# One more probability chunk turned by DMA in a graph-attention kernel, with its buffers, score sums and row statistics rearranged

## The reference

```python
# layer 0
anchor_adj = jnp.einsum('md,de,ne->mn', x, weight, input)       # 6144 x 6144
scores = jnp.where(adj > 0, anchor_adj, NEG_PAD)
l0 = softmax(scores / 0.07, axis=1) @ input
x = layernorm(x + l0)
# layer 1
Wh = x @ W;  s1 = Wh @ a1;  s2 = Wh @ a2
e = leaky_relu(s1[:, None] + s2[None, :], 0.2)
h = softmax(where(adj > 0, e, -9e15), axis=1) @ Wh
x = layernorm(x + elu(h))
```

## Time and profile before

| | |
|---|---|
| profiled execution | 1458.37 us |
| its span | 1456.6 us |
| PE busy | 1411.4 us, 97% |
| VectorE busy | 1253.8 us, 86% |
| ScalarE busy | 1066.9 us, 73% |
| GpSimd busy | 1217.3 us, 84% |
| granted TensorE clock, mean of the span | 0.989 |
| DMA, mean | 200 GB/s; in stage 1 about 265 GB/s |

### The profile page before, as it was taken

The page is one execution under the profiler, slowest core; times in us unless marked ns, Lnnn a source line. Parts: engine busy times, 40 slices in busy tenths (PEclk is TensorE's granted clock), DMA queues, the critical chain, the costliest instruction groups (busy, mean ns, idle before and its releaser), DMA issues.

```text
span 1456.6 us, 28346 instructions
## 1 busy us (share of the span) xinstructions
PE 1411.4 (97%) x9661; PEld 1010.5 (69%) x9661; DVE 1253.8 (86%) x2129; ACT 1066.9 (73%) x2435; POOL 1217.3 (84%) x906
## 2 busy tenths in 40 slices
PE   8799999999999999999999999979999999999995
PEld 4577777777777777777777777755666666666664
DVE  6799999999999899999999999849898897979794
ACT  6688888888888888888888888868755555545453
POOL 6978888888888888888888888838999999999995
PEclk9999999999999999999999999988999999999998
DMA  8799999999999999999999998673434343434420
GB/s 267 243 286 261 271 253 266 273 266 275 273 256 264 249 272 267 270 271 271 266 256 265 261 261 268 185 140 66 107 68 103 85 102 85 104 67 111 76 58 14
DMA packets 427918, 291.38 MB, mean 200 GB/s; under 512 B 356864, under 2 KB 403200, under 8 KB 427776
## 3 DMA queue, kind: packets, MB, share of 16 engines
q1 hardware_dynamic: 427776, 289.59, 73.0%
HBM read 160.56 MB, written 40.89 MB: 138 GB/s over the span
## 4 chain that ended last, share of the span: by engine, by line
PE 92%; DVE 2%; POOL 2%; issue 1%; ACT 1%; DMA 1%; SPq 0%; POOLq 0%; ACTq 0%; DVEq 0%
PE ps L594 16%; PE ps L680 13%; PE ps L673 12%; PE ps L620 11%; PE ps L596 8%; PE ps L633 8%; PE ps L632 8%; PE ps L631 8%; PE ps L657 6%; PE ps L691 1%; POOL edges L426 1%; PE ps L564 1%; DVE rows L934 1%; POOL inp_sb L416 1%; POOL vals L419 0%
## 5 line engine op out<-in xcount | busy, mean ns | idle before, releaser
L798 ACT ACTIVATE rows<-rows,exp_bias 128x512 f32<-128x512 f32 x576 | 417.2, 724 | 58.2 <-DVE exp_bias L987 58.2
L505 POOL TENSOR_TENSOR p_lo<-p,p_hi 128x1024 fp32r<-128x1024 f32 x180 | 423.7, 2395 | 21.8 <-ACT p_hi L832 11.5
L934 DVE CUSTOM_DVE_ANT_0 rows<-ps,neg_mask 128x1024 f32<-128x1024 f32 x288 | 352.2, 1223 | 81.9 <-PE ps L633 71.1
L1014 DVE SCALAR_TENSOR_TENSOR p<-ps,e_col,edgesT 128x1024 f32<-128x1024 f32 x288 | 349.6, 1276 | 53.4 <-PE ps L650 36.5
L426 POOL TENSOR_SCALAR edges<-neg_mask 128x1536 uint8<-128x1536 bf16 x192 | 311.2, 1621 | 92.7 <-DVE neg_mask L909 80.7
L832 ACT CAST p_hi<-p 128x1024 fp32r<-128x1024 f32 x180 | 185.1, 1047 | 166.5 <-DVE p L1014 163.9
L594 PE MATMUL ps<-vals,pT_hi 128*128 128x256 f16 x1536 | 295.9, 273 | 3.1 <-DVE pT_lo L943 2.1
L784 ACT CAST pT_hi<-ps 128x512 f16<-128x512 f32 x384 | 222.7, 580 | 93.2 <-PE ps L620 93.0
L457 POOL TENSOR_TENSOR inp_sb<-rows,inp_sb 128x512 f16<-128x512 f32 x192 | 279.5, 1475 | 10.5 <-ACT inp_sb L792 2.9
L596 PE MATMUL ps<-vals,pT_lo 128*128 128x128 f16 x1536 | 275.1, 219 | 0.0
L943 DVE TENSOR_TENSOR pT_lo<-ps,pT_hi 128x512 f16<-128x512 f32 x384 | 250.8, 683 | 11.7 <-ACT pT_hi L784 11.7
(11 more groups left out here) (110 smaller groups left out, 1853.1 us busy)
## 6 DMA issues: line engine op xcount, KB each, us to landing
adj_sb<-adj SPq DMA_DIRECT2D x192, 768.0 KB, 5.7
edge_rows<-edges SPq DMA_DIRECT2D x192, 192.0 KB, 4.8
xq<-x SPq DMA_DIRECT2D x48, 64.0 KB, 2.9
xr<-x SPq DMA_DIRECT2D x48, 64.0 KB, 5.8
out<-y_w SPq DMA_DIRECT2D x5, 512.0 KB, 3.6
inp_sb<-inp SPq DMA_DIRECT2D x3, 768.0 KB, 8.2
inp_sb<-inp_sb SPq DMA_TRANSPOSE x96, 4.7
edgesT<-edge_rows SPq DMA_TRANSPOSE x48, 5.3
```

The source lines that it names most:

```text
L505: nc.gpsimd.tensor_tensor(p1_lo[:, m % LO_SLOTS, :], p1[:, (NB * g + n) % P_SLOTS, :], p1_hi[:, m % HI_SLOTS, :].bitcast(F32), ALU.subtrac ...
L798: nc.scalar.activation(row_chunk(1 - par, c), row_chunk(1 - par, c), ACT.Exp, bias=exp_bias[:, 1 - par:2 - par], scale=EXP_SCALE, accum_ou ...
L934: nc.vector.tensor_tensor_reduce(row_pair(par, k), scores_pair(k), neg_mask_row[:, 2 * k * CHUNK:2 * (k + 1) * CHUNK], 1.0, -3.0e38, ALU.a ...
L1014: nc.vector.scalar_tensor_tensor(out=p1[:, (NB * g + n) % P_SLOTS, :], in0=ps[:, R_ROW:R_ROW + 2, :].rearrange("p b w -> p (b w)"), scalar ...
```

## The change

- `MOVED` goes from 4 to 5: five of twelve chunks are split in SBUF and turned by DMA, seven by TensorE.
- `movedT` has one set instead of two. It is filled in two parts, chunks 0 to 2 and chunks 3 and 4, each with its own semaphore, so SP issues four DMA transposes a tile instead of two. Each part waits until TensorE has used the same chunks of the tile before.
- GpSimd makes a fifth low half, between the edges of quarters 0 and 1 of the next tile.
- GpSimd no longer multiplies `x1` by the weight rows and ScalarE no longer sums the products. VectorE does both in two instructions a tile, at step 7 (`SUMS_STEP`).
- `x1_total` is gone. TensorE sums all `x1` rows itself, one product of width 1 a tile, 46 of them in call t = 48.
- VectorE takes the row statistics of a tile at step 0 of the next call. GpSimd's power and `x1` move to the start of its next call. For the last tile VectorE does the two additions and `x1`.

```diff
-MOVED = 4
+MOVED = 5
+MOVED_PARTS = ((0, 3), (3, 5))
-        movedT = inp_space[:, 2 * MW:6 * MW].rearrange("p (s h b m) -> p s h b m", s=2, h=2, m=P)
+        movedT = inp_space[:, 2 * MW:4 * MW].rearrange("p (h b m) -> p h b m", h=2, m=P)
@@ SyncE
-                    after(sp, pv_done, C * (tile - 1))
-                    sp.dma_start_transpose(movedT[:, par, 0], moved_hi).then_inc(movedT_in[par], 16)
-                    sp.wait_ge(moved_lo_set, MOVED * (tile + 1))
-                    sp.dma_start_transpose(movedT[:, par, 1], moved_lo).then_inc(movedT_in[par], 16)
+                    for k, (a, b) in enumerate(MOVED_PARTS):
+                        after(sp, pv_done, C * (tile - 1) + (C - MOVED) + b if tile >= 1 else 0)
+                        for half, of, ready in ((0, moved_hi, moved_hi_set), (1, moved_lo, moved_lo_set)):
+                            sp.wait_ge(ready, MOVED * tile + b)
+                            sp.dma_start_transpose(movedT[:, half, a * BPC:b * BPC, :], of[:, a * CHUNK:b * CHUNK]
+                                                   ).then_inc(movedT_in[k], 16)
@@ GpSimd
+            def rstd_of_tile(tile):
+                pool.wait_ge(ve_set, tile + 1)
+                nc.gpsimd.tensor_tensor(small[:, 4:5], small[:, 3:4], consts[:, 0:1], ALU.pow).then_inc(rstd_set, 1)
             def tile_rstd(t, par, known):
+                if t >= 3:
+                    tile = t - 3
+                    rstd_of_tile(tile)
+                    pool.wait_ge(rstd_set, tile + 1)
+                    nc.gpsimd.tensor_scalar(x1_all[:, tile, :], xr[:, 1 - par, :], moments[:, 0:1], small[:, 4:5], ALU.subtract,
+                                            ALU.mult).then_inc(x1_set, 1)
...
+                if moved:
+                    moved_low(t - 1, 4)
+                if ahead:
                     make_edges(t + 1, 1)
...
-                    pool.wait_ge(ve_set, tile + 1)
...
-                    score_cols(tile)
@@ TensorE
+            def mean_part(j):
+                pe.wait_ge(x1_set, j + 1)
+                return nc.tensor.matmul(mean_ps, x1_all[:, j, :], averager[:, 0:1], start=(j == 0), stop=(j == NB - 1),
+                                        skip_group_check=True)
             def tile_steps(t, par, known):
                 for c in range(C):
+                    if t == NB:
+                        for j in range(4 * c, min(4 * c + 4, NB - 2)):
+                            mean_part(j)
@@ VectorE
+            def row_statistics(tile):
+                dve.wait_ge(u_set, tile + 1)
...
+            def score_sums(j):
+                dve.wait_ge(x1_set, j + 1)
+                dve.wait_ge(wa_copied, 1)
+                after(dve, s_set, 2 * j)
+                for k in range(2):
+                    nc.vector.tensor_tensor_reduce(s_prod[:, k, :], x1_all[:, j, :], wa_rep[:, k, :], 1.0, 0.0, ALU.mult,
+                                                   ALU.add, s_cols[:, k, j:j + 1]).then_inc(s_set, 1)
             def tile_steps(t, par, known):
                 for c in range(C):
+                    if c == 0 and t >= 3:
+                        row_statistics(t - 3)
...
+                    if c == SUMS_STEP and t >= 3:
+                        score_sums(t - 3)
```

More of the change, by code:

```diff
@@ L156, in build @@
         SPARE = EX0
-        VALS_BANKS = (2, 3, OUT3)
+        VALS_BANKS = (2, 3, SPARE)
+        mean_ps = ps[:, OUT3, 3 * P:3 * P + 1]
         def vals1_ps(k):
@@ L225, in build @@
         moved_hi_set, moved_lo_set = sem("moved_hi_set"), sem("moved_lo_set")
-        movedT_in = [sem(f"movedT_in{i}") for i in range(2)]
+        movedT_in = [sem(f"movedT_in{i}") for i in range(len(MOVED_PARTS))]
         att_out = sem("att_out")
@@ L285, in movedT_loads, with moved_part @@
         def movedT_loads(tile):
-            return 32 * (tile // 2 + 1)
+            return 32 * (tile + 1)
+        def moved_part(i):
+            return next(k for k, (a, b) in enumerate(MOVED_PARTS) if a <= i < b)
         def tiles(eng, body):
@@ L490, in tile_rstd @@
                     nc.gpsimd.tensor_tensor(xr[:, par, :], att[:, P:2 * P], xr[:, par, :], ALU.add).then_inc(u_set, 1)
-                    pool.wait_ge(ve_set, tile + 1)
[L492 to L495, removed]
-                    score_cols(tile)
             tiles(pool, tile_rstd)
+            rstd_of_tile(NB - 1)
             def low_part(g, n):
@@ L753, in _ @@
             z_high(1)
-            def score_sums(j):
-                act.wait_ge(s_prod_set, j + 1)
-                for k in range(2):
-                    op = nc.scalar.activation(s_prod[:, k, :], s_prod[:, k, :], ACT.Copy, accum_out=s_cols[:, k, j:j + 1])
-                op.then_inc(s_set, 1)
             def tile_steps(t, par, known):
@@ L901, in xT_low @@
                                                in1=xT_hi[:, par, :], op0=ALU.mult, op1=ALU.subtract).then_inc(xT_lo_set, 1)
+            def row_statistics(tile):
+                dve.wait_ge(u_set, tile + 1)
+                after(dve, x1_set, tile)
+                nc.vector.bn_stats(stats[:], xr[:, tile % 2, :]).then_inc(stats_set, 1)
+                dve.wait_ge(stats_set, tile + 1)
+                nc.vector.bn_aggr(moments[:], stats[:]).then_inc(moments_set, 1)
+                dve.wait_ge(moments_set, tile + 1)
+                nc.vector.tensor_scalar(small[:, 3:4], moments[:, 1:2], EPS, None, ALU.add).then_inc(ve_set, 1)
+            def score_sums(j):
[5 more added lines that the diff above has]
+                                                   ALU.add, s_cols[:, k, j:j + 1]).then_inc(s_set, 1)
             def make_mask(t, q, known):
@@ L970, in tile_steps @@
                                                     ALU.mult).then_inc(scaled_set, 1)
[L971 to L979 removed]
+                        if c == ATT_STEP + 1 and t == NB + 1:
+                            dve.wait_ge(att_out, NB)
+                            dve.wait_ge(xr_in[par], 16 * (t // 2))
+                            nc.vector.tensor_tensor(xr[:, par, :], att[:, 0:P], xr[:, par, :], ALU.add).then_inc(u1_set, 1)
+                            dve.wait_ge(u1_set, NB)
+                            nc.vector.tensor_tensor(xr[:, par, :], att[:, P:2 * P], xr[:, par, :], ALU.add).then_inc(u_set, 1)
                     if c == C - 1 and scores_of(known):
@@ L990, in _ @@
             tiles(dve, tile_steps)
-            dve.wait_ge(s_set, NB)
+            row_statistics(NB - 1)
+            dve.wait_ge(rstd_set, NB)
+            nc.vector.tensor_scalar(x1_all[:, NB - 1, :], xr[:, (NB - 1) % 2, :], moments[:, 0:1], small[:, 4:5], ALU.subtract,
+                                    ALU.mult).then_inc(x1_set, 1)
+            score_sums(NB - 1)
+            dve.wait_ge(s_set, 2 * NB)
             nc.vector.reduce_max(s_top[:, 0:1], s_cols[:, 0, :], AX_X).then_inc(s_part, 1)
```

59 lines of the change are left out of this document (17 added, 42 removed).

## The result

The changed kernel took 1487.42 us (median of 4 runs, 1486.24 to 1488.53), the kernel before 1458.35 us beside it (4 runs, 1456.67 to 1458.68): ratio 1.0201, interval 1.0187 to 1.0215. That is 29 us slower, where 1502 (1460 to 1528) had been forecast. The profiled execution has a span of 1486.6 us, 30.0 more than before.

The account below looks back on a forecast made before the run. A VectorE-GpSimd loop, nearly equal to TensorE's 19.35 us tile, would set the pace: 18.93 - 0.25 + 1.20 + 0.38 = 20.26. 1458.4 + 41 (45 tiles) + 3 (end of stage 1) = 1502 us, range 1460 to 1528.

Parts of the forecast that it names:

- the loop GpSimd, VectorE, GpSimd: Stage 1: edges to additions, statistics to mask, edges again; 18.93 us alone, 20.26 a tile after the change.
- The signs that were named for it: Middle tile: edges 20.2 us apart, VectorE idle over 1 us before statistics, TensorE gap at step 2, GpSimd chain 15.1 to 15.5.
- Statistics not opened by the move, row maximum ahead: VectorE's statistics still wait for GpSimd's additions; row maximum and bias go ahead of them, -0.25 us a tile.
- the slack: Free time in the loop of the kernel before: 0.42 us a tile of 19.35.
- The fifth low half: GpSimd, between mask and additions: adds its bare 1.20 us to the loop; could be 1.5 with stretching.
- The score sums: VectorE's two sums at step 7 hold up GpSimd's low halves: 0.38 us a tile, ends 0 and 0.56.
- The rate taken from the masks: VectorE masks stretch GpSimd by 0.68 us per us of mask; applied to 0.56 us of score sums.
- End of stage 1: Calls 48 and 49 and the chain to stage 2: +4.5, +0.7 and -2, together +3 us, between 0 and +5.
- TensorE as the limit: Rival: the loop has unseen slack, TensorE still sets stage 1's tile at 18.91 us; 1442 us; chance 0.13.
- VectorE held up by the sums: Rival: score sums wait for GpSimd instructions, VectorE sets the tile at about 20.8 us; 1526 us; chance 0.18.
- VectorE's busy time: In the rival with VectorE as limit: 17.6 + 2.7 = 20.3 us a tile, with waits about 20.8.
- The DMA: Rival: DMA or SP's queue is late, masks wait for `adj`; tile 20.3 to 20.8, 1505 to 1525 us; chance 0.08.

Follow-up runs that it names:

- Run 1: Changed kernel with GpSimd's fifth low half moved behind the two additions: 1457.02 us, ratio 0.9988 to the kernel before.
- run 3: Kernel before with one more GpSimd subtraction of 128x512 a tile, ahead of the fourth low half, its result unread: 1493.98 us, ratio 1.0245.
- run 7: Changed kernel with the old score path (GpSimd product, ScalarE sums) and GpSimd's running sum back, fifth low half left in place: 1474.36 us, ratio 1.0108.
- run 2: Changed kernel with four chunks turned by DMA instead of five, in parts of two and two, all else kept: 1560.52 us, ratio 1.0705.
- run 5: Changed kernel with four DMA chunks and the old score path and GpSimd's running sum back: 1456.0 us, ratio 0.9984.
- run 6: Changed kernel, five chunks, with the fifth low half behind the additions and the old score path and running sum back: 1439.42 us, ratio 0.9868.
- Run 4: Kernel before with one more GpSimd subtraction of 128x128 a tile, ahead of the fourth low half, its result unread: 1459.68 us, ratio 1.0017.

## Why the prediction was right

*What bounds the kernel.* Right: the loop GpSimd, VectorE, GpSimd, hidden behind a TensorE at 100%, took over. Run 1 opened it and the 30 us went; run 3 lengthened it in the kernel before and the time rose by 36 us. The signs that were named for it are there: VectorE idles 1.04 us ahead of the statistics, TensorE's gap is at the transposes of step 2, GpSimd's chain is 15.18 us. But the tile is 19.87, not 20.2, at the lower end of what the sum allowed (19.88, with the score sums at nothing).

*Statistics not opened by the move, row maximum ahead.* Direction right, size too small: -0.25 was forecast, the stretch from the statistics to the edges fell by 0.55 from run 3 (5.21 to 4.66 us), since the wait for ScalarE went as well. Against this stands the slack, taken as 0.42 and measured as 0.23: the loop alone was 19.12, not 18.93. The two errors cancel but for 0.11 us, and that is luck.

*The fifth low half.* 1.20 forecast; the row shows 1.16 and 0.08 of gap, 1.24. It was not stretched.

*The score sums.* This is the term that was mis-sized: 0.38 us a tile forecast, 0.12 measured (run 7). The rate taken from the masks, 0.68 us of GpSimd's time for each us, is not one: what counts is which engine's instruction starts first. The one that starts second is longer by what is left of the first, less 0.14 us. The masks follow that too (1.08, 1.30 and 1.62 us with 0.27, 0.49 and 0.81 left of GpSimd's instruction). In the ordinary tile the first sum meets only the last 0.26 us of the edges, and the second, 0.28 long, goes 0.01 ahead of the low half and delays it by 0.13. A sum that starts inside a low half takes 0.5 to 0.95 us more than its bare length. Together with late masks this makes the two long tiles of the changed kernel, 2 us each; in run 2 every tile is 2.3 us longer than in run 5.

The sum by measured terms: 19.12 - 0.55 + 1.24 + 0.07 = 19.88, the tile of 19.87; 0.07 is the growth of the low halves from 3.06 to 3.13, of which the sums make 0.13 and a smaller stretch by the mask -0.06. The forecast was 20.26. 45 x 0.39 = 17.6 us too much, 3.9 of it given back by the two long tiles.

*End of stage 1.* Forecast +3 (5.2 in calls 48 and 49, -2 behind them); measured +3.4 and -1.8. Four of the 46 products take 0.87 us (977.53 to 978.40), so all take 10.0 us, not 12.0. What was not forecast are +1.9 at the start and +1.0 in stage 2; their causes are open. VectorE waits 1.63 us for a load of `adj` at 72.44, but run 5 waits 2.0 us at the same place and is not behind at call 3.

*The rivals.* TensorE as the limit came true only with the low half moved and the scores taken back (run 6). VectorE held up by the sums was 18 in 100 and did not happen here, apart from two tiles; run 2 shows it at 1560 us, beyond the 1526 worked out for it. VectorE's busy time came out as worked out (20.2 us a tile, 20.3 forecast); its waits were taken as 0.5 and are 1.4. The DMA was no limit of the changed kernel: no engine waits for a transfer in its tiles. Run 6 moves 288 GB/s at a share of 1.04 and TensorE never waits in the middle, though there and in run 1 single loads of `adj` come up to 0.5 and 1.1 us too late for VectorE.

## What to carry to other kernels

An engine at 100% can hide a loop through two others that is 0.2 us shorter than the tile; look for a chain without gaps that returns to its own start, and ask of each added instruction whether it stands in it. The same low half cost 30 us ahead of the two additions and nothing behind them. For the pairs of VectorE and GpSimd instructions that contend here, the cost of one depends on which starts first, and by how much, not on a rate: a kernel can stand a few tenths of a microsecond from a different regime, so a part of a change that looks harmless should be timed in more than one alignment.

## What was not expected of the hardware

- A VectorE product-and-sum with two inputs in SBUF, 0.28 us bare, takes up to 1.24 us when it starts during a GpSimd subtraction of 1.16 us, and ends 0.15 us after it. This agrees with the rule of the Trainium skill, page "SBUF — State Buffer" (Who interferes with whom), that two SBUF inputs suffice, which no row before the change could show.
- One formula gives all these lengths: bare length, plus what is left of the other engine's instruction at the start (for an instruction of GpSimd: of a mask or sum), less 0.14 us. Bare are 0.95 us for a mask and 0.28 for a sum on VectorE, 1.47 for edges and 1.16 for a low half on GpSimd. Between 90 and 940 us of all eleven traces it fits each of the 2316 masks and sums within 0.06 us, and all but four of 4095 edges and 512-column subtractions; in those four both engines' instructions start within 0.01 us of each other. VectorE's subtraction with one input in PSUM (`pT_lo`) stays at 0.67 to 0.69 us beside anything.
- It also explains why a GpSimd subtraction of 128x128 in place of 128x512 took 1.14 us instead of 1.88 (runs 4 and 3), while 128x128 additions alone take 0.46. Both start under a mask with about 0.85 us left. Run 4:

```profile
519.87 1.12 DVE L913 TENSOR_SCALAR neg_mask<-adj_sb 128x1536 bf16<-128x1536 int32 x1
520.14 1.14 POOL L477 TENSOR_TENSOR scratch<-rows,inp_sb 128x128 f16<-128x128 f32 x1
```

- A DMA share of 1.00 in the windows view is not a ceiling. Run 4 has 1.05 at 302 GB/s, and in that stretch no engine waits for a transfer:

```profile
70.00:110.00 40.00, 38.97 (x333) 29.00 (x331) 36.84 (x68) 33.96 (x89) 32.03 (x30) 1.00 1.05 302
```

Elsewhere, at 281 to 300 GB/s, single loads of `adj` did come late: by 0.3 to 0.5 us three times in run 6, by up to 1.08 us in run 1, and once early in the changed kernel (1.63 us, at 72.44).
